# Vector norms of queries and keys in a six-layer local-attention stack, taken for each eight heads by themselves

## The chip, the cores and the metric

The kernel runs on one core of one Trainium2 chip. Its time is the device time of one execution in microseconds (us); the median of several runs is given. The core has a matrix engine (TensorE, PE in the profile, with its weight loads as PEld), VectorE (DVE), ScalarE (ACT), GpSimd (POOL) and a queue for transfers (SyncE, SP). They run side by side and wait for each other by semaphores.

## What is computed

A row of stages: two small attention stages with a quantised feed-forward between them, and then six "layers", each an attention with 16 heads of 64 elements over a window of 32 tokens, and a feed-forward. There are 2048 tokens of 128 elements. The change lies in the attention of the six layers:

```python
def l2norm(t):
    return t / jnp.maximum(jnp.linalg.norm(t, axis=-1, keepdims=True), 1e-12)

def attn_layer(x, Wqkv, qs, ksc, Wo):
    qkv = x @ Wqkv
    q, k, v = jnp.split(qkv, 3, -1)          # each [tokens, 16 heads, 64]
    q = l2norm(q) * qs
    k = l2norm(k) * ksc
    ...
    q = q * cos * scale + rotate_half(q) * sin * scale
    k = k * cos * inv + rotate_half(k) * sin * inv
    out = local_attention(q, k, v)           # softmax over the window
    return out @ Wo
```

## The kernel before

Everything is float32, except for a few masks. The 2048 tokens of a layer are taken in 16 tiles T of 128 tokens (one token in each partition). For each tile there are queries (i = 0) and keys (i = 1), 16 heads of 64, so 1024 columns; they come out of the matrix product as two banks b = 0 and 1 of PSUM, with eight heads (512 columns) each. Five layers run in a hardware loop, the sixth (l = 5) is written out behind it, without registers for the semaphore counts. Each engine has its own list of instructions, in an order written out by hand, and works it off strictly in that order.

The way of one tile's queries or keys is this (lines of the kernel before):

- `project` (L1264, PE): two products into banks 0 and 1. It waits for the `normalise` of what stood in the bank before (semaphore `qn`, bank by bank).
- `squares` (L1485, ACT): each bank squared into `square`, half by half.
- `sum_squares` (L1644, DVE): for each half, the sums over 64 elements into `norm[:, 0]`. Semaphore `total` counts halves.
- `inverse_norms` (L1491, L1493, L1495, ACT): when both halves are summed, three functions of [128, 16] values: Relu(n - 1e-24), Ln, and Exp(-0.5 x); it leaves one over the norm in `norm[:, 2]`. Relu and the constant added within Ln keep the norm from falling under 1e-12. Each waits for the one ahead of it (semaphore `root`, three counts).
- `normalise` (L1655, DVE): after `root` has all three counts, for each half a product of the bank and the inverse norm, broadcast over 64 elements, into `qn`. Both halves stand directly behind each other.
- `cosines` (L1663, DVE), `rotate` (L1201, L1202, and for queries L1208, POOL) and `add_rotated` (keys, L1671, DVE): the rotary embedding, into `hat`.
- `turn` (L1280, PE) transposes `hat` in four parts r = 0 to 3 (two of the queries, two of the keys), `store_qk` (L1508 to L1515, ACT) copies them out of PSUM, and part 3 uses the bank of part 0, so it waits for part 0's copy. `scores` (L1298), `maxima` and `subtract` (L1677, L1683, DVE), `exponentials` (L1523, ACT), `sums` (L1690, L1692, DVE), `normalise_weights` (L1225, POOL), `turn_weights` (L1313, PE), `place_low` (L1530, L1531, ACT) and `place_high` (L1699, DVE), `values` (L1332, PE), `store_o` (L1539, ACT), `out_project` (L1344, PE) and `residual` (L1708, DVE) follow.

The iteration of tile T works ahead: it takes the keys of T + 1 and the queries of T + 2 through their norms. In it the orders are:

- DVE: residual(T-2); sum_squares(keys); place_high(T-1); **normalise(keys)**; maxima; subtract; sum_squares(queries); cosines(keys); add_rotated(keys); sums; **normalise(queries)**; cosines(queries).
- ACT: store_qk, 4 parts; squares(keys); place_low(T-1, 0); **inverse_norms(keys)**; place_low(T-1, 1); store_o, 2 parts; squares(queries); exponentials; **inverse_norms(queries)**; store_values (L1499).
- PE: turn parts 0, 1; out_project(T-2); turn parts 2, 3; project(keys, T+1); turn_weights(T-1); scores(T), 2 parts; values(T-1, 0); values(T-1, 1); project(queries, T+2); project(values, T+1).

values(T-1, 1) waits for place_low(T-1, 1) (semaphore `low`), which stands behind inverse_norms(keys) on ACT. In a layer's second half, `forward`, PE works through the feed-forward, and the norms of the next layer's first tiles (queries and keys of tile 0, queries of tile 1) are taken between; the last of these stands on DVE just ahead of `add_output` (L1762), for whose result the first tile's turn (part 1) waits. At the start of the first layer the same three norms are taken one after another.

Of the kernel before, what the change touches and what calls it, by code (L numbers as in the profile page):

```python
# [10 lines left out]
ALU = mybir.AluOpType  # L11
ACT = mybir.ActivationFunctionType
AX = mybir.AxisListType

P = 128
N = 2048
NT = N // P
# [4 lines left out]
EPS = 1e-5  # L22
# [1023 lines left out]
LD = 64  # L1046
LH = 16
HALF = LH // 2
# [7 lines left out]
LN_RANGE = 2.0 ** 24  # L1056
NORM_MIN = 1e-12
START = 1
# [17 lines left out]
def layers(nc, t, a):  # L1076
# [4 lines left out]
    with ExitStack() as ctx:  # L1081
# [4 lines left out]
        X, ps = t.X, t.ps  # L1086
# [11 lines left out]
        norm = sb("norm", [P, 3, LH])  # L1098
        qn = sb("qn", [P, 2, LH, LD])
# [29 lines left out]
        with nc.Block() as block:  # L1129
# [345 lines left out]
            def _(e):  # L1475
# [12 lines left out]
                def inverse_norms(l, T, i):  # L1488
                    n = (l * NT + T) * 2 + i
                    e.wait_ge(s.total, START + 2 * n + 2)  # L1490
                    e.activation(norm[:, 1, :], norm[:, 0, :], ACT.Relu, bias=const[:, 4:5]).then_inc(s.root, 1)  # L1491
                    e.wait_ge(s.root, 3 * n + 1)
                    e.activation(norm[:, 1, :], norm[:, 1, :], ACT.Ln, bias=const[:, 0:1], scale=LN_RANGE).then_inc(s.root, 1)  # L1493
                    e.wait_ge(s.root, 3 * n + 2)
                    e.activation(norm[:, 2, :], norm[:, 1, :], ACT.Exp, bias=const[:, 1:2], scale=-0.5).then_inc(s.root, 1)  # L1495
# [138 lines left out]
            def _(e):  # L1634
# [11 lines left out]
                def normalise(l, T, i):  # L1646
                    n = (l * NT + T) * 2 + i
                    e.wait_ge(s.root, 3 * n + 3)
                    if T:
                        e.wait_ge(s.rotated, START + (n - 2) * 3 + (2 if i else 3))  # L1650
                    else:
                        e.wait_ge(s.rotated, START + l * (6 * NT))
                    for b in range(2):
                        heads = slice(HALF * b, HALF * (b + 1))
                        e.tensor_tensor(qn[:, i, heads, :], ps[:, b, :].rearrange("p (h d) -> p h d", h=HALF),  # L1655
                                        norm[:, 2, heads].unsqueeze(2).to_broadcast([P, HALF, LD]), ALU.mult).then_inc(s.qn, 1)
# [160 lines left out]
def tables():  # L1817
# [29 lines left out]
    const = np.zeros((P, 5), np.float32)  # L1847
    const[:, 4] = -NORM_MIN ** 2
    const[:, 0], const[:, 1], const[:, 2] = NORM_MIN ** 2 * LN_RANGE, 0.5 * np.log(LN_RANGE), EPS
# [10 lines left out]
def program(nc, a, out):  # L1860
    with ExitStack() as outer:
# [17 lines left out]
        t.const = t.early[:, SCALES + 4 * LD:SCALES + 4 * LD + 5]  # L1879
# [71 lines left out]
```

## Time and profile before

| what | us |
|---|---|
| median of 3 runs | 3179.58 |
| lowest and highest of them | 3169.4, 3195.48 |
| the profiled execution, device time | 3166.38 |
| its span from first to last instruction | 3164.6 |
| PE busy in it | 2810.0 (89%) |
| DVE busy | 2600.2 (82%) |
| ACT busy | 2207.2 (70%) |
| POOL busy | 1358.5 (43%) |

The six layers lie from about 1340 us to the end. A row of the timeline gives the start in us, the duration in us, the engine, the line, the operation, what it writes and reads, how many instructions are merged in the row, and in brackets how long the engine had been idle before and which instruction's end released it. A row of groups gives busy us and the mean ns of one instruction behind the bar.

### The profile page before, as it was taken

The page shows a single profiled execution, that of the slowest core. Times are in us where ns is not written, and L with a number is a line of the kernel's source. Part 1 is how long each engine was busy: PE and PEld are TensorE (multiplying, and loading weights), DVE is VectorE, ACT ScalarE, POOL GpSimd, SP SyncE. Part 2 cuts the span into 40 slices and gives each one's busy share as a digit, 9 for nine tenths or more (in the row PEclk, how much of TensorE's full clock was granted, in tenths as well). Part 3 has the DMA queues.
Part 4 walks back from the last instruction along what each step waited for, and adds up shares of the span by engine and source line. Part 5 has one row for each costly group of instructions (what it writes and reads, how often), then busy time and mean ns, then how long its engine had stood idle before and what let it go on. Part 6 is the DMA issues. An engine that isn't in the chain of part 4 may idle for free. (4 is left out here: it accounts for less than half of the span.)

```text
span 3164.6 us, 74279 instructions
## 1 busy us (share of the span) xinstructions
PE 2810.0 (89%) x29085; PEld 1575.4 (50%) x29181; DVE 2600.2 (82%) x3866; ACT 2207.2 (70%) x3498; POOL 1358.5 (43%) x818
## 2 busy tenths in 40 slices
PE   3999898998988789779998998998899899998998
PEld 1233333333433333356656664666467657655764
DVE  4999889888788779379968995998699779968995
ACT  2377777677666667668867876887688668867884
POOL 0200433424224210066636663666466546645661
PEclk8699999999999999889999999999999999999999
DMA  3200001010010210011111111111111111111110
GB/s 113 67 2 1 1 8 31 1 38 1 9 32 2 46 42 2 11 35 35 35 49 36 35 35 43 42 35 56 29 35 35 56 29 35 38 46 35 37 39 21
DMA packets 62995, 101.21 MB, mean 32 GB/s; under 512 B 20450, under 2 KB 45216, under 8 KB 61472
## 3 DMA queue, kind: packets, MB, share of 16 engines
q1 hardware_dynamic: 62636, 96.26, 11.2%
q8 instruction: 245, 4.01, 0.5%
q14 instruction: 114, 0.93, 0.1%
HBM read 38.30 MB, written 7.34 MB: 14 GB/s over the span
## 5 line engine op out<-in xcount | busy, mean ns | idle before, releaser
L914 DVE TENSOR_REDUCE a_part<-ps 128x1 f32<-128x512 f32 (+3 forms) x1664 | 985.4, 652 | 155.4 <-PE ps L594 148.5
L890 ACT ACTIVATE a_Pb<-ps 128x1024 f32<-128x1024 f32 (+3 forms) x832 | 762.8, 974 | 348.3 <-PE ps L760 346.9
L1264 PE MATMUL ps<-early 128*128 128x512 f32 x1152 | 563.5, 623 | 89.1 <-DVE l_qn L1655 70.7
L1201 POOL TENSOR_TENSOR l_sine<-l_qn,stack 128x512 f32<-128x512 f32 x192 | 344.2, 1793 | 220.9 <-DVE l_qn L1655 213.6
L1225 POOL TENSOR_TENSOR l_weights<-l_weights,l_rcp 128x1024 f32<-128x1024 f32 x96 | 182.5, 1901 | 495.9 <-DVE l_rcp L1692 495.9
L594 PE MATMUL ps<-stack,a_QS 48*128 48x512 bf16 x1024 | 313.2, 405 | 74.0 <-DMA a_QS<-pieces 32.0
L1264 PEld LDWEIGHTS ps<-early 128*128 128x128 f32 x1152 | 207.7, 194 | 317.1 <-issue 130.5
L1644 DVE TENSOR_REDUCE l_norm<-l_square 128x8 f32<-128x512 f32 x384 | 253.6, 683 | 100.4 <-ACT l_square L1485 92.5
L1485 ACT ACTIVATE l_square<-ps 128x512 f32<-128x512 f32 x384 | 228.0, 596 | 107.1 <-PE ps L1264 102.4
L1655 DVE TENSOR_TENSOR l_qn<-ps,l_norm 128x512 f32<-128x512 f32 x384 | 246.5, 684 | 56.5 <-ACT l_norm L1495 56.1
L1663 DVE TENSOR_TENSOR l_cosine<-l_qn,stack 128x1024 f32<-128x1024 f32 x192 | 286.3, 1491 | 4.1
L644 PE MATMUL ps<-a_Pb,V 128*32 128x256 f32 (+1 forms) x3968 | 280.1, 399 | 0.0
L594 PEld LDWEIGHTS ps<-stack,a_QS 48*128 48x128 bf16 x1024 | 76.0, 94 | 346.7 <-DVE a_part L914 266.3
L1202 POOL TENSOR_TENSOR l_sine<-l_qn,stack 128x512 f32<-128x512 f32 x192 | 243.1, 1266 | 0.0
L1208 POOL TENSOR_TENSOR l_hat<-l_cosine,l_sine 128x1024 f32<-128x1024 f32 x96 | 227.3, 2368 | 22.1 <-POOL l_sine L1202 19.1
L1298 PE MATMUL ps<-l_kT,l_qT 128*64 128x64 f32 x6144 | 221.2, 225 | 14.0
L1280 PE MATMUL ps<-ident,l_hat 128*128 128x128 f32 x1536 | 205.9, 278 | 23.1 <-DVE early L1762 7.5
L493 POOL TENSOR_TENSOR a_xc<-x,a_stat 128x512 f32<-128x512 f32 x12 | 12.5, 1038 | 488.0 <-DVE a_stat L971 488.0
L1298 PEld LDWEIGHTS ps<-l_kT,l_qT 128*64 128x64 f32 x6144 | 194.8, 138 | 54.5 <-issue 54.5
L1280 PEld LDWEIGHTS ps<-ident,l_hat 128*128 128x128 f32 x1536 | 180.6, 143 | 79.2 <-issue 65.4
L1332 PE MATMUL ps<-l_wT,l_V_earlier 128*64 128x64 f32 x3072 | 193.2, 225 | 3.0 <-ACT l_wT L1531 2.4
L1344 PE MATMUL ps<-l_oT,l_w_o 128*128 128x128 f32 x1536 | 188.2, 276 | 4.1 <-ACT l_oT L1539 4.1
(215 smaller groups left out, 5001.5 us busy)
## 6 DMA issues: line engine op xcount, KB each, us to landing
l_V_earlier<-l_V SPq DMA_DIRECT2D x96, 384.0 KB, 3.5
l_V_earlier<-l_V SPq DMA_DIRECT2D x96, 128.0 KB, 3.3
early<-in_L_ffn_Wqkv_dram SPq DMA_DIRECT2D x6, 1536.0 KB, 8.2
a_QS<-pieces SPq DMA_DIRECT2D x96, 64.0 KB
pieces<-a_piece SPq DMA_DIRECT2D x6, 512.0 KB, 2.6
pieces<-early SPq DMA_DIRECT2D x12, 256.0 KB, 2.7
a_KS<-pieces SPq DMA_DIRECT2D x48, 64.0 KB
l_w_o<-in_L_ffn_Wo_dram SPq DMA_DIRECT2D x6, 512.0 KB, 4.0
```

Source lines behind the costliest of these rows:

```text
L594: mm = e.matmul(bank[:, 0:width], QS[rows, c, pair, qt * P:(qt + 1) * P], KS[A][rows, pair, b * CH:b * CH + width], start=not masked, stop ...
L644: mm = e.matmul(O[32 * h:32 * h + 32, lo:hi], V[A][:, kt, at:at + 32], Pb[:, n % 2, h, lo:hi], start=(kt == 0), stop=(kt == tiles_of(u) - ...
L890: e.activation(Pb[:, n % 2, 2 * p:2 * p + 2, lo:CH], ps[:, 2 * p:2 * p + 2, lo:CH], ACT.Exp)\
L914: e.tensor_reduce(part[:, u % 2, column(h, qt), b:b + 1], bank[:, 0:width], AX.X, ALU.max)\
L1201: e.tensor_tensor(sine[:, :, 0:ROT], swap[:, :, ROT:LD], table[:, :, 0:ROT], ALU.mult).then_inc(s.rotated, 1)
L1202: e.tensor_tensor(sine[:, :, ROT:LD], swap[:, :, 0:ROT], table[:, :, ROT:LD], ALU.mult).then_inc(s.rotated, 1)
L1264: e.matmul(ps[:, (V_BANK[T] if i == 2 else 0) + b, :], XS[:, T * P:(T + 1) * P], w_qkv[:, at:at + CH], start=True, stop=True).then_inc(s.v ...
L1280: tr = e.transpose(ps[:, TURN_BANK[r], j * P:(j + 1) * P], hat[:, i, at:at + P], t.ident[:, :])
L1298: mm = e.matmul(ps[half:half + LD, bank, at:at + LD], qT[:, T % 2, j, w, :, :], kT[:, T % 2, j, WIN * w:WIN * (w + 2)], start=False, stop= ...
L1644: e.tensor_reduce(norm[:, 0, heads], square[:, heads, :], AX.X, ALU.add).then_inc(s.total, 1)
L1655: e.tensor_tensor(qn[:, i, heads, :], ps[:, b, :].rearrange("p (h d) -> p h d", h=HALF), norm[:, 2, heads].unsqueeze(2).to_broadcast([P, H ...
L1663: e.tensor_tensor(cosine[:, i, :, :], qn[:, i, :, :], tab[:, 2 * i, T, :].unsqueeze(1).to_broadcast([P, LH, LD]), ALU.mult).then_inc(s.cos ...
```

## The change

The three functions for all 16 heads become two functions for each eight heads: Ln and Exp of a half follow as soon as that half is summed. Relu is gone. The norm's lower bound is kept in `normalise`: its product becomes one instruction with two operations, min(inverse norm, 1e12) times the bank, with the bound given as a constant of the instruction. Each half's product waits for its own half's Exp. Semaphore `root` counts four per norm in place of three. The small number added within Ln becomes 1e-33 in place of 1e-24, and the constant that Relu used is dropped from the table of constants.

```diff
                 def inverse_norms(l, T, i):
-                    n = (l * NT + T) * 2 + i
-                    e.wait_ge(s.total, START + 2 * n + 2)
-                    e.activation(norm[:, 1, :], norm[:, 0, :], ACT.Relu, bias=const[:, 4:5]).then_inc(s.root, 1)
-                    e.wait_ge(s.root, 3 * n + 1)
-                    e.activation(norm[:, 1, :], norm[:, 1, :], ACT.Ln, bias=const[:, 0:1], scale=LN_RANGE).then_inc(s.root, 1)
-                    e.wait_ge(s.root, 3 * n + 2)
-                    e.activation(norm[:, 2, :], norm[:, 1, :], ACT.Exp, bias=const[:, 1:2], scale=-0.5).then_inc(s.root, 1)
+                    for b in range(2):
+                        n = ((l * NT + T) * 2 + i) * 2 + b
+                        heads = slice(HALF * b, HALF * (b + 1))
+                        e.wait_ge(s.total, START + n + 1)
+                        e.activation(norm[:, 1, heads], norm[:, 0, heads], ACT.Ln, bias=const[:, 0:1], scale=LN_RANGE).then_inc(s.root, 1)
+                        e.wait_ge(s.root, 2 * n + 1)
+                        e.activation(norm[:, 2, heads], norm[:, 1, heads], ACT.Exp, bias=const[:, 1:2], scale=-0.5).then_inc(s.root, 1)
...
                 def normalise(l, T, i):
                     n = (l * NT + T) * 2 + i
-                    e.wait_ge(s.root, 3 * n + 3)
...
                     for b in range(2):
                         heads = slice(HALF * b, HALF * (b + 1))
-                        e.tensor_tensor(qn[:, i, heads, :], ps[:, b, :].rearrange("p (h d) -> p h d", h=HALF),
-                                        norm[:, 2, heads].unsqueeze(2).to_broadcast([P, HALF, LD]), ALU.mult).then_inc(s.qn, 1)
+                        e.wait_ge(s.root, 4 * n + 2 * b + 2)
+                        e.scalar_tensor_tensor(out=qn[:, i, heads, :], in0=norm[:, 2, heads].unsqueeze(2).to_broadcast([P, HALF, LD]),
+                                               scalar=1.0 / NORM_MIN, in1=ps[:, b, :].rearrange("p (h d) -> p h d", h=HALF),
+                                               op0=ALU.min, op1=ALU.mult).then_inc(s.qn, 1)
```

The order on ScalarE in an iteration, around the keys' norms (`l_norm`), between the two parts of `place_low` (`l_wT`). Before:

```order
L1531 COPY l_wT<-ps 64x16x32
L1490 REGISTER_ALU
L1491 ACTIVATE l_norm<-l_norm,early 128x16
L1492 ISA
L1493 ACTIVATE l_norm<-l_norm,early 128x16
L1494 REGISTER_ALU
L1495 ACTIVATE l_norm<-l_norm,early 128x16
L1528 REGISTER_ALU
L1530 COPY l_wT<-ps 64x16x32
```

and now, at the same place:

```order
L1532 COPY l_wT<-ps 64x16x32
L1493 REGISTER_ALU
L1494 ACTIVATE l_norm<-l_norm,early 128x8
L1495 ISA
L1496 ACTIVATE l_norm<-l_norm,early 128x8
L1493 REGISTER_ALU
L1494 ACTIVATE l_norm<-l_norm,early 128x8
L1495 ISA
L1496 ACTIVATE l_norm<-l_norm,early 128x8
L1529 REGISTER_ALU
L1531 COPY l_wT<-ps 64x16x32
```

Three functions of 16 values have become four of 8 values; nothing else in the queue has moved. The same holds for the queries' norms, behind `exponentials`.

The order on VectorE in an iteration, from `place_high` (`l_wT`) over the keys' `normalise` (`l_qn`) to `maxima` and `subtract`. Before:

```order
L1699 COPY l_wT<-ps 64x16x32
L1648 ISA
L1650 ISA
L1655 TENSOR_TENSOR l_qn<-ps,l_norm 128x512 x2
L1676 REGISTER_ALU
L1677 TENSOR_REDUCE l_nmax<-ps 128x16
L1683 TENSOR_TENSOR l_weights<-ps,l_nmax 128x1024
```

and now:

```order
L1701 COPY l_wT<-ps 64x16x32
L1650 ISA
L1655 ISA
L1656 SCALAR_TENSOR_TENSOR l_qn<-l_norm,ps 128x512
L1655 REGISTER_ALU
L1656 SCALAR_TENSOR_TENSOR l_qn<-l_norm,ps 128x512
L1678 REGISTER_ALU
L1679 TENSOR_REDUCE l_nmax<-ps 128x16
L1685 TENSOR_TENSOR l_weights<-ps,l_nmax 128x1024
```

The two products have become instructions with two operations, and the second has a wait of its own ahead of it. No instruction has changed its place.

## Rows read from the trace of the kernel before

**Rows 1.** The page's first line.

```profile
span 3164.6 us, 74279 instructions
```

**Rows 2.** Stretches: their length, busy us per engine, granted PE clock, DMA share.

```profile
1699.80:1715.27 15.47, 14.59 (x184) 10.78 (x183) 14.24 (x19) 12.47 (x25) 10.21 (x6) 1.00 0.12 36
1683.00:1700.00 17.00, 15.94 (x181) 11.23 (x182) 13.86 (x17) 12.41 (x25) 10.20 (x6) 0.90 0.24 62
```

**Rows 3.** Timeline of one iteration (T = 2, second layer), all engines, cut.

```profile
1701.02 1.99 PE L1264 MATMUL ps<-early 128*128 128x512 f32 x4 [0.73 <-DVE l_qn L1655]
...
1703.89 1.28 DVE L1644 TENSOR_REDUCE l_norm<-l_square 128x8 f32<-128x512 f32 x2
...
1705.20 0.31 ACT L1491 ACTIVATE l_norm<-l_norm,early 128x16 f32<-128x16 f32 x1 [1.10 <-DVE l_norm L1644]
...
1705.88 0.31 ACT L1495 ACTIVATE l_norm<-l_norm,early 128x16 f32<-128x16 f32 x1
...
1706.33 1.29 DVE L1655 TENSOR_TENSOR l_qn<-ps,l_norm 128x512 f32<-128x512 f32 x2 [0.44 <-ACT l_norm L1495]
...
1706.81 0.58 ACT L1531 COPY l_wT<-ps 64x512 f32<-64x512 f32 x1
...
1707.17 0.20 PEld L1332 LDWEIGHTS ps<-l_wT,l_V 128*64 128x64 f32 x4
...
1707.44 0.20 PEld L1332 LDWEIGHTS ps<-l_wT,l_V_earlier 128*64 128x64 f32 x4
...
1710.40 0.69 DVE L1644 TENSOR_REDUCE l_norm<-l_square 128x8 f32<-128x512 f32 x1 [0.39 <-ACT l_square L1485]
...
1716.49 0.70 PE L1264 MATMUL ps<-early 128*128 128x512 f32 x1 [0.73 <-DVE l_qn L1655]
```

**Rows 4.** Timeline at the same seam of `values`: tile 14, then the sixth layer.

```profile
1606.37 0.20 PEld L1332 LDWEIGHTS ps<-l_wT,l_V 128*64 128x64 f32 x4
1606.48 0.20 PEld L1332 LDWEIGHTS ps<-l_wT,l_V_earlier 128*64 128x64 f32 x4
...
2966.88 0.20 PEld L1332 LDWEIGHTS ps<-l_wT,l_V 128*64 128x64 f32 x4
...
2967.27 0.20 PEld L1332 LDWEIGHTS ps<-l_wT,l_V_earlier 128*64 128x64 f32 x4 [0.18 <-ACT l_wT L1531]
```

**Rows 5.** Timeline of the first iteration (T = 0) of the second layer.

```profile
1673.58 1.15 PE L1298 MATMUL ps<-l_kT,l_qT 128*64 128x64 f32 x32
...
1674.55 1.29 DVE L1655 TENSOR_TENSOR l_qn<-ps,l_norm 128x512 f32<-128x512 f32 x2 [1.17 <-ACT l_norm L1495]
```

**Rows 6.** Timeline at the seam from the first layer to the second.

```profile
1663.19 0.69 DVE L1655 TENSOR_TENSOR l_qn<-ps,l_norm 128x512 f32<-128x512 f32 x1 [1.17 <-ACT l_norm L1495]
...
1667.32 0.47 PE L1280 MATMUL ps<-ident,l_hat 128*128 128x128 f32 x1 [1.84 <-DVE early L1762]
```

**Rows 7.** Timeline of the first norm ahead of the first layer.

```profile
1346.93 0.69 DVE L1655 TENSOR_TENSOR l_qn<-ps,l_norm 128x512 f32<-128x512 f32 x1 [1.05 <-ACT l_norm L1495]
```

**Rows 8.** Groups on VectorE by line and shape: busy us, mean ns, idle before.

```profile
L1655 DVE TENSOR_TENSOR l_qn<-ps,l_norm 128x512 f32<-128x512 f32 x384 | 246.5, 684 | 56.5 <-ACT l_norm L1495 56.1 <-POOL l_sine L1202 0.4
L1751 DVE SCALAR_TENSOR_TENSOR l_weights<-ps,l_b,l_gelu 128x512 f32<-128x512 f32 x48 | 35.9, 749 | 22.8 <-ACT l_gelu L1591 12.4 <-PE ps L1415 10.0
...
L1769 DVE SCALAR_TENSOR_TENSOR l_xn<-l_xn,l_vec,l_cosine 128x512 f32<-128x512 f32 x24 | 18.0, 748 | 14.8 <-ACT l_cosine L1551 14.8
...
L1772 DVE TENSOR_SCALAR l_xn<-l_xn,l_vec 128x512 f32<-128x512 f32 x24 | 11.7, 486 | 0.8
...
L151 DVE TENSOR_SCALAR a_wrot<-a_wall 128x128 f32<-128x128 f32 x1 | 0.2, 230 | 0.0
...
L47 DVE TENSOR_SCALAR stat<-stat 128x16 f32<-128x16 f32 x1 | 0.2, 175 | 0.0
```

**Rows 9.** Groups on ScalarE by line and shape: busy us, mean ns, idle before.

```profile
L1495 ACT ACTIVATE l_norm<-l_norm,early 128x16 f32<-128x16 f32 x192 | 59.1, 308 | 6.2
...
L844 ACT ACTIVATE a_stat<-a_stat 128x4 f32<-128x4 f32 x12 | 2.5, 205 | 3.6 <-DVE a_stat L977 3.6
```

More of the change, by code:

```diff
@@ L1057 @@
 NORM_MIN = 1e-12
+LN_FLOOR = NORM_MIN ** 2 * 1e-9
 START = 1
@@ L1846, in tables @@
     mask_c = np.stack([np.tile(low(seen), (1, 8)), np.tile(np.concatenate([low(seen0), low(seen)], 1), (1, 4))], 1)
-    const = np.zeros((P, 5), np.float32)
-    const[:, 4] = -NORM_MIN ** 2
-    const[:, 0], const[:, 1], const[:, 2] = NORM_MIN ** 2 * LN_RANGE, 0.5 * np.log(LN_RANGE), EPS
+    const = np.zeros((P, 4), np.float32)
+    const[:, 0], const[:, 1], const[:, 2] = LN_FLOOR * LN_RANGE, 0.5 * np.log(LN_RANGE), EPS
     const[:, 3] = growth[i % LD] ** (CH // (WIN // 2))
@@ L1878, in program @@
         t.scales = t.early[:, SCALES:SCALES + 4 * LD].rearrange("p (i d) -> p i d", i=4)
-        t.const = t.early[:, SCALES + 4 * LD:SCALES + 4 * LD + 5]
+        t.const = t.early[:, SCALES + 4 * LD:SCALES + 4 * LD + 4]
         t.ps = outer.enter_context(nc.psum_tensor("ps", [P, 8, CH], F32))
```

## Prediction

> **What bounds the kernel now.** The page's span is 3164.6 us [rows 1], and 96 iterations of about 15.5 us in six layers make almost half of it, so I read one iteration before anything else. The stretch view of T = 2 in the second layer (first row of [rows 2]) shows PE busy for 14.59 of 15.47 us, VectorE for 14.24, ScalarE for 12.47: two engines are nearly full, and neither is quite. Such a pattern is a ring in which two engines wait for each other in turn. So the next view is the timeline of that iteration, read for its brackets [rows 3]:
>
> - PE begins the keys' product at 1701.02, after 0.73 us idle, released by `l_qn`, the queries' `normalise` at the end of the iteration before.
> - VectorE sums the keys' squares from 1703.89. ScalarE had been idle for 1.10 us when these sums released it, and runs Relu, Ln and Exp from 1705.20, one every 0.34 us (1705.20, then Exp at 1705.88), so to 1706.19.
> - VectorE stands idle for 0.44 us until Exp is done, and starts the keys' `normalise` at 1706.33.
> - ScalarE's two copies of `place_low` come behind Exp, and the last ends at 1706.81 + 0.58 = 1707.39. PE's `values` has to wait for it: one group of weight loads starts at 1707.17, the next, the first that needs the copy, at 1707.44.
> - PE then runs on to the queries' product. Its square releases VectorE at 1710.40, after 0.39 us idle.
> - The next keys' product starts at 1716.49, again released by `l_qn` after 0.73 us: the period is 15.47 us.
>
> The ring that closes is thus: queries' sums on VectorE (1710.40) to queries' `normalise`, PE from 1701.02 (1716.49) through `values` to the queries' product, ScalarE's square, VectorE. The 0.44 us stall at the keys' `normalise` is **not** in this ring: VectorE, released 0.44 us sooner, comes to the queries' sums sooner and waits 0.83 us there instead of 0.39. What is in the ring is the place where PE waits for `place_low`, and that hangs on Exp.
>
> How long PE waits there is read from the spacing of the weight-load groups [rows 4]. In tile 14, where no norm stands ahead of the copies, the seam between the two parts is 0.11 us (1606.37 to 1606.48), as between any two groups. In the steady iteration it is 0.27, so 0.16 us are lost. In the sixth layer, which has no registers to work out, PE comes sooner and the seam is 0.39 (2966.88 to 2967.27, the bracket names `l_wT`): 0.28 us lost.
>
> **The change part by part.**
>
> *ScalarE's chain.* The first half is summed about 0.69 us after 1703.89, at 1704.58; Ln and Exp of it take 2 x 0.34 us, to about 1705.25. The second half is summed at 1705.17, so its Ln starts near 1705.27 and its Exp ends near 1705.91, against 1706.19. An activation of 8 values lies between 205 ns (4 values and no bias taken from SBUF) and 308 ns (16 values) [rows 9]; I take 300, since the bias stays. So `place_low` comes 0.28 us sooner, enough for the 0.16 and just enough for the 0.28. From below: if the functions took 0.34 us each with a further 0.1 between halves, 0.18 us would still remain.
>
> *In the iterations.* 13 tiles per layer (T = 1 to 13) have this seam with a norm ahead of it. Five layers: 65 x 0.16 = 10.4 us. Sixth: 13 x 0.28 = 3.6 us.
>
> *At T = 0.* There VectorE idles 1.17 us ahead of the keys' `normalise` [rows 5], and `maxima` comes right behind it, released by scores that PE has ended at 1673.58 + 1.15 = 1674.73. Now `normalise` may start at once behind the sums: Exp of the first half is ready while the second is summed, and Exp of the second (0.67 us behind its sums) while the first product runs (0.69). It would end at 1673.4 + 1.3 = 1674.7, and `maxima` start at 1674.8 where it now starts at 1674.55 + 1.2 = 1675.75. Nothing else covers this, as PE's product of values waits for `subtract`: 6 x 0.95 = 5.7 us.
>
> *At the seam of two layers.* The last norm ahead of `add_output` costs VectorE 1.17 us idle, and PE stands idle for 1.84 us until `add_output` is done [rows 6]. All but 0.04 of the 1.17 should go; I take 1.0 for what PE sees: 5 x 1.0 = 5.0 us. The other two norms in each `forward` lie beside PE's feed-forward, which runs through, and are worth nothing.
>
> *At the start.* Three norms one behind the other, each with 1.05 us idle ahead of its product (the first is in [rows 7]); 0.9 each: 2.7 us.
>
> *ScalarE's extra function.* Behind `exponentials` the queries' norm takes four functions for three, +0.33 us, which pushes `store_values` and the first copy of `store_qk`, for which `turn` part 3 waits. What hides it is PE's 0.73 us idle behind `turn` [rows 3]; without it, it would be 0.33 us per iteration. So nothing.
>
> *The product.* Before, 684 ns [rows 8]. With two operations and a scalar read from SBUF for each partition, 749 (L1751) and 748 (L1769). The new one's scalar is a constant. What a scalar from SBUF costs is read from the one-tensor form: with constants 175 ns at 16 columns (L47) and 230 at 128 (L151), so 0.49 ns a column and 418 at 512; with scalars from SBUF it is 486 (L1772), 68 more. Taking these 68 off 749 leaves 681: the new instruction costs as much as the old. Bounds: 0, and +0.065 us. Only the queries' first half is in the ring (78 x 0.065 = 5.1 us), and both halves at the 14 single places (1.8 us): at most 6.9 us.
>
> **Sum:** 10.4 + 3.6 + 5.7 + 5.0 + 2.7 = 27.4 us less, of the profiled execution's 3164.6 us, and 20.5 with the dearer product. That execution (3166.38 with what lies around its span) is 13 us under the median of the runs, 3179.58; nothing here scales with that difference, so I take 27 off the median: 3153 us. T = 14 (one stall of 0.44 us each, at most 2.6 in six layers) and T = 15 (no norm in it) I leave at nothing.
>
> **A rule that speaks against it.** The two-source form L1769 reads two float32 tensors from SBUF in 748 ns, and L1751 one from PSUM and one from SBUF in 749: the source does not matter [rows 8]. The Trainium skill, page "Vector Engine (DVE) Microarchitecture Reference", section "Points that are easy to get wrong", says that this form "with two non-bf16 SBUF sources halves throughput"; the rows don't agree, and here only one source is in SBUF. By that rule 512 columns would cost as much as 1024.
>
> **The rivals.**
>
> 1. *The whole stall comes off.* If the ring ran through the keys' `normalise`, each iteration would lose 0.44 us: 78 x 0.44 = 34.3, with the single places 13.4, so 48 us: 3132. For it: VectorE's 14.24 busy of 15.47. Against it: its 0.39 us idle behind the stall, with another releaser. 0.12.
> 2. *Only the single places.* If PE's own sequencer, and not the copy, made the 0.27 us seam, the iterations keep their 15.47: 13.4 us less, 3166. For it: the view shows no bracket at 1707.44. Against it: 1707.44 is 0.05 us behind the copy's end, as in the sixth layer, where the bracket stands. 0.15.
> 3. *Slower: ScalarE's queue becomes the bound.* If the four functions for three are not hidden, +0.33 us in each of 78 iterations, 25.7, less 13.4 of the single places: +12, 3192. Its place is `turn` part 3 behind the first copy; it decides once the copy comes more than the 0.73 us later that PE has idle. 0.05.
> 4. *Slower: the product runs at half rate.* A second pass costs at most what the first does, 0.68 us: 78 x 0.68 = 53, less 27: +26, 3206. Its place is the queries' first product, ahead of PE's; it decides once that product costs 0.35 us more than now (27.4 / 78). The 748 and 749 of the two-operation rows speak against it. 0.03.
> 5. *The clock.* In the second layer T = 1 takes 17.00 us at a granted clock of 0.90 (second row of [rows 2]) against 15.47 at 1.00, behind a stretch with PE idle. If the moved waits put this into each layer, up to 1.5 x 4 = 6 us come back: 3159. 0.05. It may as well vanish.
>
> **Numbers.** The forecast, 3153, has 0.60. The range runs from rival 1 to past rival 2: 3130 to 3174; outside lie rivals 3 and 4 and the tails from the spread of the runs, which is 26 us over three. One per cent is 32 us, about what a measurement can tell from no change. Faster by more: rival 1 and a fifth of the forecast, 0.24. Slower by more: only what the spread adds to rivals 3 and 4, 0.05. Within: 0.71.
>
> **What the changed profile would show.** Idle of VectorE ahead of `l_qn` down from 56.5 us [rows 8] to a few; the seam in `values` 0.11 us in all layers; the period 15.3 in five layers and 15.15 in the sixth; VectorE's idle ahead of the queries' sums up to some 0.7 us; the product at 680 to 690 ns, not 749; the Exp near 0.30. I am wrong if the seam closes and the period stays (something else ends the wait on the ring), if PE's 0.73 us idle turns into a wait for ScalarE, or if the single places don't come forward together with their norm.

## The result, and the profile after

The changed kernel has a median of 3143.35 us over four runs (3135.21 to 3149.84); the kernel before, measured with it, 3178.15 us (3169.4 to 3195.48). The ratio is 0.9894, with a 95% interval from 0.9873 to 0.9916. That is 34 to 35 us less, where 27 were forecast, and inside the range of 3130 to 3174. Two more measurements of the same pair, further down, gave 0.9926 (0.9900 to 0.9952) and 0.9925 (0.9899 to 0.9952), so that the change brings 0.7 to 1.1%, or 23 to 34 us. The first result is the best of the three.

From the page of the changed kernel's profiled execution, its first line and the line with each engine's busy us, share of the span and number of instructions:

```profile
span 3133.4 us, 74866 instructions
PE 2802.7 (89%) x29085; PEld 1564.2 (50%) x29181; DVE 2594.8 (83%) x3866; ACT 2238.7 (71%) x3690; POOL 1365.0 (44%) x818
```

The span is 31.2 us under the 3164.6 of [rows 1]. Here is the same iteration as in [rows 3] (T = 2 of the second layer) in the changed kernel's timeline; columns are start, length, engine, line, operation, and in brackets the idle time before it and what ended it. Most lines of the code stand one further down than before.

```profile
1692.00 1.99 PE L1265 MATMUL ps<-early 128*128 128x512 f32 x4 [0.66 <-DVE l_qn L1656]
...
1694.89 1.28 DVE L1645 TENSOR_REDUCE l_norm<-l_square 128x8 f32<-128x512 f32 x2
...
1695.61 0.30 ACT L1494 ACTIVATE l_norm<-l_norm,early 128x8 f32<-128x8 f32 x1 [0.52 <-DVE l_norm L1645]
...
1696.20 0.69 DVE L1701 COPY l_wT<-ps 64x512 f32<-64x512 f32 x1
...
1696.53 0.30 ACT L1496 ACTIVATE l_norm<-l_norm,early 128x8 f32<-128x8 f32 x1
1696.86 0.58 ACT L1531 COPY l_wT<-ps 64x512 f32<-64x512 f32 x1
1696.92 1.28 DVE L1656 SCALAR_TENSOR_TENSOR l_qn<-l_norm,ps 128x512 f32<-128x512 f32 x2
...
1697.45 0.58 ACT L1532 COPY l_wT<-ps 64x512 f32<-64x512 f32 x1
...
1698.15 0.20 PEld L1333 LDWEIGHTS ps<-l_wT,l_V 128*64 128x64 f32 x4
...
1698.27 0.20 PEld L1333 LDWEIGHTS ps<-l_wT,l_V_earlier 128*64 128x64 f32 x4
...
1701.25 1.45 DVE L1645 TENSOR_REDUCE l_norm<-l_square 128x8 f32<-128x512 f32 x2 [0.65 <-ACT l_square L1486]
...
1707.32 1.99 PE L1265 MATMUL ps<-early 128*128 128x512 f32 x4 [0.67 <-DVE l_qn L1656]
```

Read it against [rows 3]. ScalarE begins Ln at 1695.61, while VectorE still sums the second half, and its last Exp ends at 1696.83, 1.94 us behind the start of the sums; before it was 1706.19 - 1703.89 = 2.30. The second copy of `place_low` ends at 1697.45 + 0.58 = 1698.03, which is 6.03 us behind the start of the keys' product on PE; before, 1707.39 - 1701.02 = 6.37. The weight group that needs it starts at 1698.27, 0.12 behind the group before: the 0.27 us seam is gone. The keys' `normalise` at 1696.92 follows VectorE's copy without a stall, and VectorE now idles 0.65 us ahead of the queries' sums, instead of 0.39. PE's idle ahead of the keys' product is still there, 0.67 us. The period is 1707.32 - 1692.00 = 15.32 us.

The changed kernel's groups by line and shape (busy us, mean ns | idle before and its releasers), which answer to [rows 8] and [rows 9]:

```profile
L1656 DVE SCALAR_TENSOR_TENSOR l_qn<-l_norm,ps 128x512 f32<-128x512 f32 x384 | 246.1, 681 | 4.6 <-ACT l_norm L1496 0.2
...
L1645 DVE TENSOR_REDUCE l_norm<-l_square 128x8 f32<-128x512 f32 x384 | 252.8, 683 | 114.4 <-ACT l_square L1486 107.1
...
L1496 ACT ACTIVATE l_norm<-l_norm,early 128x8 f32<-128x8 f32 x384 | 115.6, 301 | 12.4
```

VectorE's idle ahead of `l_qn` fell from 56.5 us to 4.6, and the new product takes 681 ns where the old took 684. Some 34 us of the vanished 52 (78 x 0.44) stood in the iterations, and these became only 12.2 us shorter, as the table shows: most of that stall cost nothing.

To see where the 31 us lie, I took the starts of VectorE's reciprocal, one per tile, through both traces. A step from one tile's reciprocal to the next is called after the two tiles:

| stretch | before | after | gain |
|---|---|---|---|
| first layer instruction to first reciprocal | 42.4 | 36.7 | 5.7 |
| T = 0 to 1, sum of six layers | 95.1 | 93.4 | 1.7 |
| T = 1 to 13, each of five layers | 185.7 | 183.9 | 5 x 1.80 = 9.0 |
| T = 1 to 13, sixth layer | 185.1 | 181.9 | 3.2 |
| T = 13 to 15, each layer | 25.3 to 25.5 | 25.2 to 25.5 | 0.2 in all |
| T = 15 to T = 0 of the next layer, five seams | 72.3 to 73.6 | 69.4 to 70.6 | 14.4 |
| the last reciprocal to the end | 56.0 | 56.4 | -0.4 |

Together 33.7 us; the stage ahead of the layers ended 2.5 us later in this execution, which leaves 31.2. These are one trace of each kernel, and this trace of the changed kernel is its fastest: in the two later ones the layers take 3.6 and 3.9 us more, of which 3.0 lie ahead of the first reciprocal (39.7 us for 36.7) and the rest at the seams.

### The profile page after: what moved, and what is told of

Same layout as the page of the kernel before. It is cut to its first block and busy times, and to the rows that moved or that the text cites. A ratio compares the mean times of both kernels' runs of the same rounds, so it can differ in the third digit from the quotient of the medians.

```text
span 3133.4 us, 74866 instructions
## 1 busy us (share of the span) xinstructions
PE 2802.7 (89%) x29085; PEld 1564.2 (50%) x29181; DVE 2594.8 (83%) x3866; ACT 2238.7 (71%) x3690; POOL 1365.0 (44%) x818
## 5 line engine op out<-in xcount | busy, mean ns | idle before, releaser
L1265 PE MATMUL ps<-early 128*128 128x512 f32 x1152 | 555.7, 615 | 76.7 <-DVE l_qn L1656 60.1
L1202 POOL TENSOR_TENSOR l_sine<-l_qn,stack 128x512 f32<-128x512 f32 x192 | 344.1, 1792 | 201.2 <-DVE l_qn L1656 193.5
L1645 DVE TENSOR_REDUCE l_norm<-l_square 128x8 f32<-128x512 f32 x384 | 252.8, 683 | 114.4 <-ACT l_square L1486 107.1
L1656 DVE SCALAR_TENSOR_TENSOR l_qn<-l_norm,ps 128x512 f32<-128x512 f32 x384 | 246.1, 681 | 4.6 <-ACT l_norm L1496 0.2
L1203 POOL TENSOR_TENSOR l_sine<-l_qn,stack 128x512 f32<-128x512 f32 x192 | 249.5, 1299 | 0.0
L1333 PE MATMUL ps<-l_wT,l_V_earlier 128*64 128x64 f32 x3072 | 185.3, 222 | 2.4 <-ACT l_wT L1532 2.4
```

The source lines that it names most:

```text
L1202: e.tensor_tensor(sine[:, :, 0:ROT], swap[:, :, ROT:LD], table[:, :, 0:ROT], ALU.mult).then_inc(s.rotated, 1)
L1203: e.tensor_tensor(sine[:, :, ROT:LD], swap[:, :, 0:ROT], table[:, :, ROT:LD], ALU.mult).then_inc(s.rotated, 1)
L1265: e.matmul(ps[:, (V_BANK[T] if i == 2 else 0) + b, :], XS[:, T * P:(T + 1) * P], w_qkv[:, at:at + CH], start=True, stop=True).then_inc(s.v ...
L1645: e.tensor_reduce(norm[:, 0, heads], square[:, heads, :], AX.X, ALU.add).then_inc(s.total, 1)
L1656: e.scalar_tensor_tensor(out=qn[:, i, heads, :], in0=norm[:, 2, heads].unsqueeze(2).to_broadcast([P, HALF, LD]), scalar=1.0 / NORM_MIN, in ...
```

## The experiments

All kernels compute the whole of the result. "The layers" below is the time from the first instruction of the layers to the end, which leaves out the stage ahead of them: that one ends anywhere from 1340 to 1357 us, whatever the kernel. Each ratio is against the kernel before in the same set of runs. Its medians in the three later sets were 3168.55, 3180.27 and 3174.45, so medians of different sets don't compare, and the plain quotient of two medians can lie 0.2% off the ratio.

**One function fewer, but no halves.** The changed kernel with Ln and Exp of all sixteen heads behind both sums:

```diff
-                    for b in range(2):
-                        n = ((l * NT + T) * 2 + i) * 2 + b
-                        e.wait_ge(s.total, START + n + 1)
...
+                    n = (l * NT + T) * 2 + i
+                    e.wait_ge(s.total, START + 2 * n + 2)
+                    e.activation(norm[:, 1, :], norm[:, 0, :], ACT.Ln, bias=const[:, 0:1], scale=LN_RANGE)
...
```

> The changed kernel without the split by halves: Ln and Exp of all 16 heads once both halves are summed, and the bound in the product. Theory (PE's wait for the copies behind Exp sets the iterations, and the split serves only the places where VectorE's wait stands alone): Exp ends 0.34 us sooner than before, so the seam in values closes as in the changed kernel and the iterations take the same 15.32 and 15.16 us; the stall of VectorE ahead of the keys' product is 0.10 us. The single places gain 0.34 us each where the split gained about 1.1: span 3164.6 - 12.4 - about 6 = 3146, and up to 4 us either way by the clock. Rival (the split makes the gain in the iterations too): the iterations gain less than half of the 12.4 us, span 3153 or more.

Measured: 3149.57 us, ratio 0.9925 (0.9898 to 0.9953). The profiled span was 3161.4, which by itself would speak for the rival; but the stage ahead of the layers ended almost 16 us later than in the first trace of before, and the iterations decide. The twelve steps from T = 1 to 13 take 183.87 us, as in the changed kernel, and 181.93 in the sixth layer (in the loop, eleven take 15.29 and the one from T = 3 to 4 takes 15.66; why is open). So in the iterations the halves give nothing: that `place_low` comes one function (0.34 us) sooner closes the seam by itself. At the seams of the layers they do give something: 70.8 us where the clock is full, against 69.85 to 70.0. The layers took 1805.6 us, against 1790.8 in the changed kernel's first trace, but the medians of the two kernels, 3149.57 and 3148.85 of the same set, can't be told apart.

**Halves, but all three functions.** The kernel before, with Relu, Ln and Exp for each half, and the old product:

```diff
+                    for b in range(2):
+                        e.activation(norm[:, 1, heads], norm[:, 0, heads], ACT.Relu, bias=const[:, 4:5])
...
```

> The kernel before with the split alone: Relu, Ln and Exp for each eight heads, the old product with a wait for its half. Theory: the six functions are one chain of 6 x 0.34 us from the first half's sums (1704.6 in the iteration shown), so the second Exp ends 0.46 us later than before; place_low and PE's values come 0.46 us later, the period becomes 15.9 us in all layers, 78 x 0.46 = +36 us; the single places gain some 0.35 us each, about -5. Span 3195, slower than before by 1%. Rival (splitting gains by itself since VectorE may start its first product sooner): span at or under 3164.6.

Measured: 3187.74 us, ratio 1.0049 (1.0031 to 1.0067), so slower than before, with periods of 15.73 and 15.67 us. Its timeline in the second layer (ScalarE and VectorE around the keys' norm, then the queries' sums, and PE's weight loads):

```profile
1710.73 0.30 ACT L1495 ACTIVATE l_norm<-l_norm,early 128x8 f32<-128x8 f32 x1
...
1711.06 0.30 ACT L1497 ACTIVATE l_norm<-l_norm,early 128x8 f32<-128x8 f32 x1
1711.27 0.29 ACT L1493 ACTIVATE l_norm<-l_norm,early 128x8 f32<-128x8 f32 x1
...
1711.71 1.29 DVE L1657 TENSOR_TENSOR l_qn<-ps,l_norm 128x512 f32<-128x512 f32 x2
...
1713.47 0.20 PEld L1332 LDWEIGHTS ps<-l_wT,l_V_earlier 128*64 128x64 f32 x4 [0.33 <-ACT l_wT L1533]
...
1716.44 1.45 DVE L1646 TENSOR_REDUCE l_norm<-l_square 128x8 f32<-128x512 f32 x2 [1.05 <-ACT l_square L1485]
```

The stall ahead of the keys' `normalise` (1711.71) is gone, as wholly as in the changed kernel, and the iteration is 0.25 us **longer** than before. The last Exp ends at 1712.22, later than with whole functions; PE waits for the copy behind it, 0.33 us in the bracket; and VectorE has 1.05 us idle ahead of the queries' sums. What was predicted of the two places holds from the other side: VectorE's stall costs nothing, the copy's lateness costs PE. The last Exp ends 2.55 us behind the start of the sums, for 2.30 before, so 0.25 later and not the 0.46 expected. Most of that difference is the spacing of the functions: dependent ones start 0.33 apart (1710.73, 1711.06), but the first of the second half starts 0.21 behind the last of the first (1711.27).

**Only the copies moved.** The kernel before, with one call in ScalarE's order exchanged:

```diff
-                        if ahead:
-                            inverse_norms(l, T + 1, 1)
                         place_low(l, T - 1, 1)
+                        if ahead:
+                            inverse_norms(l, T + 1, 1)
```

> The kernel before, with both copies of place_low ahead of the keys' three functions in ScalarE's queue; nothing else. Theory (PE's wait is in the ring, VectorE's stall is not): the seam in values is 0.11 us, the period 15.32 us (15.16 in the sixth layer) although VectorE's stall ahead of the keys' product grows from 0.44 to about 0.55 us; the single places stay as before. Span 3164.6 - 12.4 = 3152, ratio 0.996. Rival (VectorE's stall sets the period): the period grows by 0.1 us to 15.57, span about 3172.

Measured: 3158.81 us, ratio 0.9958 (0.9933 to 0.9982). Its timeline keeps the stall in full and has the short period, 15.33 us:

```profile
1709.93 1.29 DVE L1655 TENSOR_TENSOR l_qn<-ps,l_norm 128x512 f32<-128x512 f32 x2 [0.44 <-ACT l_norm L1495]
1713.85 1.46 DVE L1644 TENSOR_REDUCE l_norm<-l_square 128x8 f32<-128x512 f32 x2 [0.24 <-ACT l_square L1485]
```

This is the cleanest verdict of the set: an edit that touches no norm gets the whole gain of the iterations (183.95 us for twelve steps, 181.93 in the sixth layer), with VectorE idle 0.44 us as ever (0.55 was expected). What the change brings beyond it lies outside the iterations: the layers take 1808.8 us here and 1790.8 to 1794.7 in the three traces of the changed kernel, of which the five seams make 11 to 12 us. The ratios of the same set, 0.9958 and 0.9926, point the same way, but their intervals overlap.

**The changed kernel again, and before again.** No edit.

> The changed kernel once more, for the granted clock around the starts of the layers. If the stretches at 1.2 GHz are a matter of the kernel's own idle times, they lie at the same places as in its first profile (second, third and fifth layer, about 10 us of stretches in all). If they fall by chance from execution to execution, they lie elsewhere, the span differs from 3133.4 by some us, and part of the difference between the two profiled spans is no effect of the change. I expect the latter, with a span between 3128 and 3142 and iterations of the same 15.32 and 15.16 us.

Measured: 3148.85 us, ratio 0.9926 (0.9900 to 0.9952), with a profiled span of 3145.2, above the 3128 to 3142 expected; the periods are the same, and the low stretches lie elsewhere. A third time:

> The changed kernel a third time, for the granted clock and the start of the layers: iterations of 15.32 and 15.16 us; stretches at the low level in other places than in its first two profiles; 1790 to 1797 us from the layers' first instruction to the end.

Measured: 3150.96 us, 0.9925 (0.9899 to 0.9952). And the kernel before:

> The kernel before once more, for the granted clock. Iterations of 15.48 and 15.43 us again. If the low stretches fall by chance, some seams between layers take 71.5 us, as the undisturbed ones did with the copies ahead of the norms, and others 72 to 73.6; the layers' start lies some us from 1340. From the layers' first instruction to the end I expect 1818 to 1826 us, against 1790.8 and 1794.4 in the two profiles of the changed kernel.

Measured: 3179.53 us, ratio to itself 1.0005 (0.9992 to 1.0019). No seam took the undisturbed 71.5 us that was expected of some: all lie at 72.3 to 73.5. The periods repeat to 0.01 us in every trace; what differs from one execution to the next is the end of the stage ahead of the layers, and where TensorE's clock is low. The stretch views below are of the kernel before in its first trace, then of the changed kernel in its first and in its third (length, busy us of PE, PEld, DVE, ACT, POOL, granted clock of 2.4 GHz, DMA share, GB/s). The stretch at 2266 us is the seam of the third and fourth layers, the one at 2545 that of the fourth and fifth:

```profile
2266.00:2269.00 3.00, 2.27 (x13) 2.09 (x14) 0.60 (x1) 2.92 (x6) 2.76 (x3) 0.78 0.01 3
```

```profile
2545.00:2548.00 3.00, 2.44 (x13) 2.43 (x14) 0.43 (x1) 2.93 (x5) 2.76 (x3) 0.65 0.01 3
```

```profile
2266.00:2269.00 3.00, 1.73 (x10) 1.49 (x9) 1.51 (x3) 2.39 (x3) 2.57 (x3) 0.67 0.03 11
```

The changed kernel's three traces are low at two, two and three seams of five, the kernel before at all five, in both of its traces. Each step to T = 1 that meets the low level (1.2 GHz) takes 17.0 us for 15.3: two of six in each trace of before, one in each of the changed kernel's. Counted from 1330 us on, the low clock lasted 69.9 and 74.4 us in the traces of before and 34.6, 50.5 and 51.2 in those of the changed kernel; of these, 33.2 and 41.0, and 20.5, 34.1 and 34.1, lie ahead of the first reciprocal. The layers took 1824.5 and 1825.0 us before, and 1790.8, 1794.4 and 1794.7 after.

**What a scalar from SBUF costs in the product.** The changed kernel with the bound read from a column of constants for the queries alone:

```diff
-                                               scalar=1.0 / NORM_MIN, in1=ps[:, b, :].rearrange("p (h d) -> p h d", h=HALF),
+                                               scalar=const[:, 4:5] if i == 0 else 1.0 / NORM_MIN, in1=ps[:, b, :].rearrange("p (h d) -> p h d", h=HALF),
```

> The changed kernel, with the bound of the queries' product read from a column in SBUF in place of the constant; the keys' product as it is. Theory (the queries' first product is in the ring, and a scalar from SBUF costs 0.065 us): the queries' product takes 749 ns, the period 15.39 us in five layers and 15.23 in the sixth, 78 x 0.065 = 5 us more than the changed kernel, and about 1 us at the single places. Rival (the product is as dear with a constant): nothing changes.

Measured: 3148.31 us, 0.9919 (0.9891 to 0.9947), period 15.39 and 15.20. The same for the keys alone (`i == 1`):

> The changed kernel, with the bound of the keys' product read from SBUF, the queries' as it is. Theory (the keys' product is off the ring, VectorE has some 0.7 us to spare behind it): the period stays at 15.32 and 15.16 us, VectorE's idle ahead of the queries' sums falls by 0.13 us, and only the single places cost about 1.5 us. Rival (VectorE as a whole is the bound): 0.13 us per iteration, period 15.45, 10 us.

Measured: 3148.26 us, 0.9908 (0.9882 to 0.9934), period 15.33 and 15.16. The medians don't separate the two; the groups and the periods do. The group rows, first with the scalar from SBUF for the queries, then for the keys (the operand `early` is that column):

```profile
L1656 DVE SCALAR_TENSOR_TENSOR l_qn<-l_norm,early,ps 128x512 f32<-128x512 f32 x192 | 134.0, 739 | 0.6
L1656 DVE SCALAR_TENSOR_TENSOR l_qn<-l_norm,ps 128x512 f32<-128x512 f32 x192 | 123.6, 685 | 3.8
```

```profile
L1656 DVE SCALAR_TENSOR_TENSOR l_qn<-l_norm,early,ps 128x512 f32<-128x512 f32 x192 | 135.2, 745 | 3.8 <-ACT l_norm L1496 0.2
L1656 DVE SCALAR_TENSOR_TENSOR l_qn<-l_norm,ps 128x512 f32<-128x512 f32 x192 | 122.6, 679 | 0.7
```

The scalar from SBUF costs 54 to 66 ns, where the prediction worked out 68. On the queries' product it is in the ring and lengthens the period by 0.07 us, and by 0.04 in the sixth layer; on the keys' it is not, and VectorE's idle ahead of the queries' sums pays for it (109.0 us for 114.4). This is the ring of the prediction, shown by putting the same cost at two places of it.

**Both edits: the change, and the copies first.**

> The changed kernel, with both copies of place_low ahead of the keys' four functions. Theory: the copies no longer wait for any norm, but in the changed kernel they already come in time for PE, so the period stays at 15.32 and 15.16 us and the seam in values at 0.11; the two remedies do not add up. VectorE's stall ahead of the keys' product comes back in part (its first half's Exp is then 0.6 us later). Rival (ScalarE's four functions still hold PE up somewhere): the period falls below 15.3.

Measured: 3149.20 us, 0.9912 (0.9880 to 0.9944), period 15.32 and 15.16, as without the move: the seam had nothing left to give.

**What fills VectorE's idle time.** The 0.65 us ahead of the queries' sums are a hole behind `subtract`, and `cosines` of the keys, ready since the keys' product, stands behind those sums. The changed kernel with one call moved on VectorE:

```diff
                         subtract(l, T)
+                        if ahead:
+                            cosines(l, T + 1, 1)
                         if T + 2 < NT:
                             sum_squares(l, T + 2, 0)
                         if ahead:
-                            cosines(l, T + 1, 1)
                             add_rotated(l, T + 1)
```

> The changed kernel, with the keys' cosines ahead of the queries' sums of squares on VectorE, in the 0.7 us that it idles there. Theory (the ring goes from the queries' sums over VectorE to the queries' product): 1.22 us less lie in the ring behind the sums, and the sums start later by what the cosines take beyond the idle time. If the cosines run at their 1.22 us, the sums start about 0.5 us later and the period falls by 0.7 us to about 14.6: 50 us less, 3090. If they have to wait for GpSimd's two sines, which run at that time, as in tile 14, where the same instruction took 2.04 us, the sums start 1.3 us later and nothing is gained: 15.3 to 15.4. I think the second more likely.

Measured: **3083.04 us, ratio 0.9710 (0.9684 to 0.9737)**: faster than both kernels, and more than I thought likely. The period is 14.47 us; in the sixth layer seven of the twelve steps take 14.26 and five 15.33. The same move in the kernel before:

> The kernel before, with the keys' cosines ahead of the queries' sums, as in the run on the changed kernel that took 14.47 us per iteration. There VectorE has no idle left in an iteration but 0.17 us, so it is the bound. Theory (VectorE's stall ahead of the keys' product was off the ring only because VectorE had time to spare): here the stall of 0.44 us is in VectorE's own chain, so the period is 14.47 + 0.44 = 14.9 us, and the change is worth 0.44 us per iteration in this order against 0.16 in the old one; 3164.6 - 78 x 0.55 = 3122, ratio 0.987. Rival (the move alone makes the gain, the norms do not matter): 14.5 us and about 3095.

Measured: 3172.68 us, 0.9987 (0.9970 to 1.0005), period 15.44: nothing, and neither the 14.9 us expected nor the rival's 14.5. The timelines tell why; first the changed kernel with the move, then the kernel before with it (VectorE, and GpSimd as POOL):

```profile
1733.43 1.25 DVE L1665 TENSOR_TENSOR l_cosine<-l_qn,stack 128x1024 f32<-128x1024 f32 x1
...
1733.56 2.26 POOL L1203 TENSOR_TENSOR l_sine<-l_qn,stack 128x512 f32<-128x512 f32 x1
...
1736.04 1.23 DVE L1673 TENSOR_TENSOR l_hat<-l_cosine,l_sine 128x1024 f32<-128x1024 f32 x1 [0.17 <-POOL l_sine L1203]
```

```profile
1721.59 1.23 DVE L1683 TENSOR_TENSOR l_weights<-ps,l_nmax 128x1024 f32<-128x1024 f32 x1
...
1722.35 1.26 POOL L1202 TENSOR_TENSOR l_sine<-l_qn,stack 128x512 f32<-128x512 f32 x1
...
1722.73 1.96 DVE L1663 TENSOR_TENSOR l_cosine<-l_qn,stack 128x1024 f32<-128x1024 f32 x1
```

`cosines` and GpSimd's second sine product come at nearly the same moment. In the first, VectorE begins 0.13 us ahead: it takes 1.25 us, and GpSimd 2.26 where it otherwise takes 1.27. In the second, the 0.44 us stall has pushed `subtract` back, GpSimd is 0.38 us ahead, and VectorE takes 1.96. The means say the same of the whole: the sine product L1203 1677 ns and `cosines` 1523 in the first, the sine 1269 and `cosines` 1784 in the second. VectorE had the time to gain, GpSimd (44% busy in the changed kernel) the time to lose.

That the order decides, and not the stall by itself, shows within one trace. In the sixth layer of the changed kernel with the move the two instructions start within 0.01 to 0.13 us of each other, and now one and now the other is first. The steps from T = 1 to 2 and from T = 2 to 3:

```profile
2824.74 1.26 POOL L1203 TENSOR_TENSOR l_sine<-l_qn,stack 128x512 f32<-128x512 f32 x1
2824.75 2.33 DVE L1665 TENSOR_TENSOR l_cosine<-l_qn,stack 128x1024 f32<-128x1024 f32 x1
...
2840.05 1.22 DVE L1665 TENSOR_TENSOR l_cosine<-l_qn,stack 128x1024 f32<-128x1024 f32 x1
2840.06 2.34 POOL L1203 TENSOR_TENSOR l_sine<-l_qn,stack 128x512 f32<-128x512 f32 x1
```

In each of the five steps in which GpSimd is first, `cosines` takes 2.22 to 2.33 us and the step 15.33, as in the kernel before with the move (15.34); in the seven in which VectorE is first, 1.22 and 14.26. So who is first is worth 0.7 us of VectorE in the loop's iterations and 1.0 to 1.1 in the sixth layer. That it is the stall, of the things in which the two kernels differ, that makes GpSimd the first in every iteration of the kernel before is read from the timelines, and was not tried alone. The Trainium skill, page "SBUF — State Buffer", section "Who interferes with whom", has this rule: a VectorE instruction with two inputs in SBUF contends with a GpSimd instruction that reads SBUF, since its second input comes through a port that the two share; the port is held exclusively, and the order of issue decides who waits. These rows agree: where VectorE is first it ends at 1733.43 + 1.25 = 1734.68, and GpSimd's 1.27 us behind that would end at 1735.95, where 1735.82 is measured. That it is this port, and nothing else that the two engines share, no run here separates.

## Why the prediction was right, and where its terms were off

- **The ring, and the stall outside it.** This is the mechanism, and it was right. The move of the copies alone kept the 0.44 us stall and had the gain; three functions by halves lost the stall and had none; the dearer product counted for the queries and not for the keys. Rival 1 (the whole stall comes off) falls with this, though a median of 3143 by itself lies between the two forecasts.
- **Iterations, 14.0 us predicted.** 12.2 measured (5 x 1.80 + 3.20). The period came out as forecast, 15.32 and 15.16. Twelve steps carry the gain, where thirteen were counted: the iteration of T = 1 has no `residual(T-2)` ahead of the keys' sums, these start 3.24 us behind the reciprocal for 3.84 at T = 2, and the seam was closed there before the change (15.32 us at full clock in both kernels). And in each of the five layers that run in the loop one step, T = 5 to 6, takes 0.1 us more, with `cosines` starting 0.11 us later there. Why stays open. Rival 2 (PE's own sequencer makes the seam) falls.
- **T = 0, 5.7 us predicted.** The step was right and a little small. From the keys' sums to the product it was 2.61 us (the sums start at 1671.94, the product as in [rows 5]), and it is now 1.39:

```profile
1664.14 1.28 DVE L1645 TENSOR_REDUCE l_norm<-l_square 128x8 f32<-128x512 f32 x2 [4.65 <-ACT l_square L1486]
...
1665.53 1.28 DVE L1656 SCALAR_TENSOR_TENSOR l_qn<-l_norm,ps 128x512 f32<-128x512 f32 x2
```

  That is 1.22 us for the predicted 0.95. Part of it is the clock: where the clock is full, as in the kernel with the copies moved, the old way takes 2.45, so that 1.06 is the change's own, and 6.4 us in six layers.
- **Seams of the layers, 5.0 us predicted from `add_output`.** The step that failed here, at four seams of five, is "I take 1.0 for what PE sees". `add_output` does come 1.07 us sooner behind the sums (1654.11 to 1657.96 in the changed kernel, 1660.74 to 1665.66 before), and PE's transposes with it. But what stands between them and the next sums is ScalarE, not PE. The changed kernel's timeline at the seam of the first two layers:

```profile
1654.11 1.28 DVE L1645 TENSOR_REDUCE l_norm<-l_square 128x8 f32<-128x512 f32 x2 [0.75 <-ACT l_square L1486]
...
1655.76 0.30 ACT L1496 ACTIVATE l_norm<-l_norm,early 128x8 f32<-128x8 f32 x1
...
1657.96 1.53 DVE L1764 SCALAR_TENSOR_TENSOR early<-ps,l_vec,early 64x512 f32<-64x512 f32 x2
1658.41 1.28 ACT L1628 ACT_TABLE_LOAD   x1 [2.35 <-issue]
...
1659.71 0.58 ACT L1509 COPY l_qT<-ps 64x512 f32<-64x512 f32 x1
...
1662.10 1.07 ACT L1512 COPY l_kT<-ps 128x512 f32<-128x512 f32 x2
...
1663.53 1.07 ACT L1486 ACTIVATE l_square<-ps 128x512 f32<-128x512 f32 x2
```

  From the table load on, ScalarE runs without a gap to the keys' square, and the load starts 2.35 us behind the last Exp, as it did before (2.33). In all traces this gap is 2.2 to 2.5 us at these four seams. So the path gains what Exp gains, 0.36 us (1.95 us behind the sums' start for 2.31), and not the stall's 1.17. With 1.06 at T = 0 this makes 1.4 us a seam. The traces agree: undisturbed seams take 71.53 us where the norms are unchanged (in the kernel with the copies moved) and 69.85 to 70.0 in the changed kernel, 1.5 to 1.7 less. The kernel with two functions of sixteen is a second test: Exp 0.35 sooner at the last norm, product 0.38 sooner at T = 0, sum 0.73; its seam is 70.78, 0.75 less.

  The fifth seam, into the layer that is written out, is another case: no table is loaded there, and ScalarE's third copy waits for PE. First the kernel before, then the changed one; the last sums ahead of `add_output` start at 2859.52 and 2835.35:

```profile
2867.18 0.58 ACT L1508 COPY l_qT<-ps 64x512 f32<-64x512 f32 x1 [2.98 <-PE ps L1280]
```

```profile
2841.49 0.58 ACT L1509 COPY l_qT<-ps 64x512 f32<-64x512 f32 x1 [2.05 <-PE ps L1281]
```

  There the predicted step holds, and the 1.07 us of `add_output` count in full. This seam gave 4.15 us of the 14.4. The clock is low at it in both traces of before, so that its undisturbed gain is an estimate, 1.07 + 1.06. For all five seams that makes 4 x 1.42 + 2.13 = 7.8 us.
- **The clock, rival 5.** Its direction was open ("it may as well vanish"), and it did nearly all of what is left. The five seams gave 14.4 us and not 7.8; in the kernel before each of them had a low stretch, and the copies of ScalarE wait 0.63 us for transposes at 1.2 GHz:

```profile
1667.26 0.58 ACT L1509 COPY l_qT<-ps 64x512 f32<-64x512 f32 x1
1667.32 2.82 PE L1280 MATMUL ps<-ident,l_hat 128*128 128x128 f32 x12 [1.84 <-DVE early L1762]
1668.46 0.58 ACT L1508 COPY l_qT<-ps 64x512 f32<-64x512 f32 x1 [0.63 <-PE ps L1280]
```

  In the changed kernel, at the seam of the next two layers, the same twelve transposes take the same 2.82 us, and the copies run back to back all the same:

```profile
1956.04 2.82 PE L1281 MATMUL ps<-ident,l_hat 128*128 128x128 f32 x12 [1.23 <-DVE early L1764]
1956.10 0.58 ACT L1509 COPY l_qT<-ps 64x512 f32<-64x512 f32 x1
...
1957.29 0.58 ACT L1509 COPY l_qT<-ps 64x512 f32<-64x512 f32 x1
```

  That seam is 70.24 us. So the 0.7 us by which PE comes sooner than ScalarE needs it are not lost: they cover the slow clock where it falls. The first trace also has one step to T = 1 at the low level fewer than before (1.7 us), and less low clock ahead of the first reciprocal. Low stretches at the seams are rarer in the changed kernel. The kernel before has one at all ten seams of its two traces, and so have its variants with three functions by halves and with `cosines` moved (ten of ten). The changed kernel has seven in fifteen, and the five experiments on it eleven in twenty-five. The kernel before with the copies moved has three in five, though its norms are the old ones, so that it isn't the norms alone; what decides stays open. Why the ratios of the three sets differ (0.9894 against 0.9925) isn't shown either; the stage ahead of the layers ends up to 13.5 us apart in the changed kernel's three traces, the layers differ by 3.9.
- **The forward norms, nothing predicted.** Nearly right: PE waited 0.33 us there for the feed-forward's product (L1424, released by L1751 at 1660.93), and that wait is gone. The path didn't go through it, as `add_output` at the end comes 1.07 us sooner and not more.
- **The start, 2.7 us predicted.** Two products of the norms there were 6.93 us apart and are now 5.79, so 1.14 us a norm and 3.4 for three. With the norm of T = 0 behind them that makes 4.5. The stretch to the first reciprocal gained 5.7 in the first traces (42.4 to 36.7), but it took 43.8 in the second trace of before and 39.7 in the two later ones of the changed kernel; the clock is at its low level over much of it in all five.
- **ScalarE's extra function.** Hidden, as said; PE's idle ahead of the keys' product stays at 0.67 us and its releaser is still `l_qn`. Rival 3 falls.
- **The product.** 681 ns, as worked out (681). Rival 4 (half rate) falls.
- **T = 13 to 15** gave 0.2 us in all: nothing, as predicted.
- **The sum.** The parts that I can lay to the change are 12.2 + 7.8 + 4.5 = 24.5 us, where 27.4 were predicted; some 9 us of the 33.7 in the first pair of traces come with the clock (an estimate, as what is left). That the first result lies above the forecast and the two later ones, 23 to 24 us, under it is thus luck with the clock and the stage ahead, and not a finer mechanism.

## What to carry to other kernels

A stall is worth what the ring pays for it: follow the work released from it to the next wait, and test the finding by moving another thing out of the ring's way, as one exchanged call did here for 0.4% (0.9958, 0.9933 to 0.9982). A stall outside the ring may still decide the order in which two engines reach a shared resource, so after taking one away look anew at what could fill the idle time: the same move was worth nothing in the kernel before and 2% in the changed one. Where several stalls end at one point, read all engines up to that point; the one that doesn't move (here a table load 2.35 us behind Exp, at four seams of five) takes over.

## What the runs showed of the hardware

- Activations that don't depend on each other overlap: with 300 ns each, one of the second half starts 0.21 us behind the last of the first, and dependent ones 0.33 to 0.34 apart.
- The form with two operations costs 681 ns at 128x512 with a constant and 739 to 745 with a scalar from SBUF; one source in PSUM and one of 8 values, spread over 64 columns each, slow nothing that these rows show (tensor product of the same size 684 ns, two tensors in SBUF 748 with a scalar from SBUF).
- Of a VectorE and a GpSimd instruction that both read two tensors of SBUF, the later waits, be it later by 0.01, 0.13 or 0.38 us: GpSimd's took 2.34 or 2.26 us for 1.27, VectorE's 2.33 or 1.96 for 1.22.
- TensorE's low clock behind a stretch of idle PE falls at different layers in each execution of the same kernel, at a price from 0.3 us (a seam where it is covered, 70.24 for 69.9) to 1.7 us (a step to T = 1). In three traces of the changed kernel with the same periods the stage ahead of the layers ended 13.5 us apart and the layers took 3.9 us more or less.
